# Products of constants in two waits of TensorE at the end of layer 1

## The reference

```python
x = x + L0_attn(layernorm(x)); x = x + L0_ffn(layernorm(x))
x = x + L1_attn(layernorm(x)); x = x + L1_ffn(layernorm(x))
x = x + L2_attn(layernorm(x)); x = x + L2_ffn(layernorm(x))
x = x + L3_attn(layernorm(x)); x = x + L3_ffn(layernorm(x))
```

```python
x1 = x @ sw1.T + sb1;  x2 = x @ sw2.T + sb2
sh = _ln(silu(x1) * x2, s_ln_g, s_ln_b)          # 64 wide
shared_out = sh @ sw3.T + sb3
x_moe = x[index_b, index_t]                      # 256 tokens
z = _ln(silu(h1) * h2, sel_ln_g, sel_ln_b)       # h1, h2: 8 experts x 64
expert_out = (z of the best expert) @ ew3
final_out = shared_out.at[index_b, index_t].set(shared_moe_out + expert_moe_out)
```

## Time and profile before

| | |
|---|---|
| median of 3 runs | 1480.39 us (1478.17 to 1481.1) |
| the profiled execution | 1478.13 us, with a span of 1476.3 us |
| mean granted clock of TensorE | 0.984 |
| busy share of the span | PE 95%, DVE 81%, ACT 75%, POOL 19% |
| PE idle ahead of L1485 (`turn`) | 8.0 us in 2 waits, the longest 4.5 us |

### The profile page before, as it was taken

One profiled execution on the slowest core, in us unless ns is written; L12 is line 12 of the kernel. 1 busy time (PEld: TensorE's weight loads), 2 busy tenths in 40 slices (PEclk: granted clock), 3 DMA queues, 4 the chain that ended last, 5 costly groups with the idle time before them and its releaser, 6 DMA issues.

```text
span 1476.3 us, 23605 instructions
## 1 busy us (share of the span) xinstructions
PE 1403.1 (95%) x8536; PEld 678.5 (46%) x8536; DVE 1191.5 (81%) x2559; ACT 1105.6 (75%) x2072; POOL 284.3 (19%) x239
## 2 busy tenths in 40 slices
PE   5989999999989978899999999999999998999997
PEld 4643333332248866233333333333333335565796
DVE  7699768583369978998788997888788767999997
ACT  3579888898867732787888888888888885887545
POOL 6212000000023322221111111110111012243542
PEclk9899999999999989999999999999999999999999
DMA  4166555655210001000000000000000000000000
GB/s 109 31 153 178 150 148 151 147 146 157 101 55 2 1 1 72 0 1 1 1 1 1 1 1 1 1 1 1 1 1 1 1 29 1 1 8 8 8 16 22
DMA packets 43620, 63.13 MB, mean 43 GB/s; under 512 B 5360, under 2 KB 25072, under 8 KB 43120
## 3 DMA queue, kind: packets, MB, share of 16 engines
q1 hardware_dynamic: 43504, 61.62, 15.4%
HBM read 54.27 MB, written 7.34 MB: 42 GB/s over the span
## 4 chain that ended last, share of the span: by engine, by line
PE 73%; DVE 15%; POOL 4%; ACT 3%; DMA 2%; issue 2%; SPq 1%; DVEq 0%; ACTq 0%
PE ps L2002 16%; PE ps L1992 13%; PE ps L525 8%; PE ps L515 7%; PE ps L1971 6%; PE ps L2012 4%; PE ps L1981 3%; DVE p6ac L2502 2%; PE ps L534 2%; POOL WA L2182 2%; PE ps L448 1%; POOL WA L2186 1%; DMA p1GB<-gscr 1%; DVE X L213 1%; PE ps L2395 1%
## 5 line engine op out<-in xcount | busy, mean ns | idle before, releaser
L2085 ACT ACTIVATE p4E<-ps,p4mx,p4sc 128x512 f32<-128x512 f32 x512 | 393.4, 773 | 108.8 <-DVE p4mx L2048 108.2
L2046 DVE TENSOR_REDUCE p4mx<-ps 128x2 f32<-128x1024 f32 x256 | 312.8, 1222 | 86.9 <-PE ps L1992 84.4
L2002 PE MATMUL ps<-p4E,p4vn 128*64 128x512 f32 x1024 | 249.2, 608 | 0.2 <-POOL p4vn L2107 0.2
L1992 PE MATMUL ps<-p4T 64*128 64x512 f16 x1536 | 211.0, 382 | 5.2 <-ACT p4E L2085 5.2
L2107 POOL TENSOR_TENSOR p4vn<-p4v,p4zs 128x512 f32<-128x512 f32 x64 | 66.7, 1042 | 480.0 <-DVE p4zs L2051 480.0
L752 ACT ACTIVATE p1g<-ps,WB 128x1024 f32<-128x1024 f32 x128 | 135.6, 1117 | 18.0 <-PE ps L515 18.0
L657 DVE SCALAR_TENSOR_TENSOR p1Pb<-ps,WB,p1GB 128x512 f32<-128x512 f32 x128 | 95.0, 748 | 65.1 <-PE ps L525 61.8
L515 PE MATMUL ps<-p1R,p1w1s 128*128 128x512 bf16 x512 | 131.7, 381 | 6.7 <-ACT xT L752 4.5
L1992 PEld LDWEIGHTS ps<-p4T 64*128 64x128 f16 x1536 | 54.7, 94 | 175.3 <-issue 105.1
L525 PE MATMUL ps<-p1g,WB 128*32 128x512 f32 x512 | 125.7, 599 | 1.8 <-DMA p1GB<-gscr 1.7
L525 PE MATMUL ps<-xn,WB 128*32 128x512 f32 x256 | 124.8, 599 | 0.0
(11 more groups left out here) (369 smaller groups left out, 2501.8 us busy)
## 6 DMA issues: line engine op xcount, KB each, us to landing
p1GB<-gscr SPq DMA_DIRECT2D x128, 256.0 KB
p1R<-tscr SPq DMA_DIRECT2D x64, 128.0 KB, 4.9
tscr<-p1tp SPq DMA_DIRECT2D x24, 128.0 KB, 3.1
WA<-in_w SPq DMA_DIRECT2D x1, 2632.0 KB, 18.8
WB<-in_w SPq DMA_DIRECT2D x1, 2560.0 KB, 9.3
X<-in_x SPq DMA_DIRECT2D x8, 256.0 KB, 5.7
gscr<-p1gT SPq DMA_DIRECT2D x8, 256.0 KB, 5.3
out<-X SPq DMA_DIRECT2D x7, 256.0 KB, 2.3
```

The source lines that it names most:

```text
L1992: y = p.e.matmul(ps[:, at + hh, :], t[rows, q, 128 * j:128 * j + 128], t[rows, 2 + r, :], start=o == 0, stop=o == 2)
L2002: t = p.e.matmul(ps[64 * hh:64 * hh + 64, self.bank["ctx", n], :], vn[n % 2][:, j, 64 * hh:64 * hh + 64], E[2 * (n % 3) + hh][:, j, :], st ...
L2046: v.e.tensor_reduce(m, ps[:, at:at + 2, :], AX, ALU.max).then_inc(v.own.h, v.one())
L2085: a.e.activation(self.E[2 * (n % 3) + hh][:, j, :], ps[:, at + hh, :], ACT.Exp, bias=self.mx[i][:, j, hh:hh + 1], scale=pre.sc[:, 1, 0:1], ...
```

## The change

Two of the steps `turn` get products of constants ahead of their wait: 37 ahead of `turn 6` and 28 ahead of `turn 8`, into the very bank that the step's transposes then write. Nothing else is altered.

```diff
             elif what == "turn":
                 self.released(p, (what, b))
+                if b in (6, NB):
+                    k.busy(p, bank[what, b], 37 if b == 6 else 28)
                 for j in range(self.src(b)[2]):
                     p.wait_ge(k.sem("us2"), 4 * b + j + 1)
                     t = p.e.transpose(ps[0:64, bank[what, b], cols(j)], self.us[i][:, j, :], k.ident)
```

## The result

| | before | after |
|---|---|---|
| median of 20 runs each | 1480.29 us (1476.08 to 1483.38) | 1475.14 us (1472.29 to 1481.22) |
| ratio, with its 95% interval | | 0.9971 (0.9961 to 0.9981) |
| span of the profiled execution | 1476.3 us | 1470.9 us |
| mean granted clock | 0.984 | 0.990 |

The ratio is 4.3 us (0.0029 x 1480.29), between 2.8 and 5.8. Forecast were 1477.3 us, 3.1 us less than before, and 0.50 for "faster by over 0.2%". It is faster, and the estimate lies above the forecast 3.1, though the interval holds 3.1 as well; its upper end, 0.9981, is just short of the 0.2% that was forecast. The two medians by themselves are 5.2 us apart. 1475.14 lies inside the range by 0.14 us, as its low end was 1475.0.

A forecast was written before the change was run, and what follows sets the result against it. Layer 1's end was taken as bound by DVE in the first wait and half-clock PE behind the second; weighted cases 0.7 + 1.75 + 0.7 = 3.1 us gave 1480.4 - 3.1 = 1477.3 us, range 1475.0 to 1480.4.

The forecast's parts named there:

- The batches and their waits: Ahead of `turn 6` and `turn 8`: products take 4.03 and 3.05 us, ending 0.6 and 1.0 us before the tiles come.
- No cost to the neighbours: DVE work during the two waits: added products slow it by 0, bounded at 0.1 us.
- The first part, 1.2 us: Between the two waits: DVE's waits of 0.44, 0.53 and 0.20 us for PE vanish, 1.2 us gained.
- The second part, 2.3 us: From `turn 8` to `back`: 1.3 us gained up to `made 0` and 1.0 in `made 0`, together 2.3 us.
- the first profile's own case: Both falls of the clock lie as first profiled and vanish: 3.5 us gained, weighted 0.5.
- The weights of the cases: Gains of 1.9, 3.5 and 4.5 us, by where the clock returns, weighted 0.35, 0.5 and 0.15: 3.1 us.
- the late return: Clock returns later than profiled, so `out 7` and `made 1` are slow too: 4.5 us gained, weighted 0.15.
- The short case: Low stretch of only 3.3 us behind the second wait, or early return behind the first: 1.9 us gained, weighted 0.35.
- It wins nothing: Rival: the chain does not wait for PE, or falls come at other places; time 1480.4 us, chance 0.08.
- the second fall stays: Rival: clock still falls around `turn 8`, with its ten transposes; time 1478.3 to 1479.2 us, chance 0.14.
- The overrun: Rival: first batch meets a low clock and ends up to 3.4 us late; time 1482.6 us, chance 0.06.
- Passed on: At `back` and after: nothing becomes late next, so the whole gain is handed on to the end.

The follow-up runs named there:

- e1: Kernel before plus only the 37 products ahead of `turn 6`, none ahead of `turn 8`: ratio 0.9981 (0.9962 to 0.9999).
- e2: Kernel before plus only the 28 products ahead of `turn 8`, none ahead of `turn 6`: ratio 0.9983 (0.9964 to 1.0002).
- e6: Kernel before plus 25 and 17 products ahead of the attention's fifth and seventh `score`, none at layer 1's end: ratio 0.9964 (0.9952 to 0.9976).
- e4: Changed kernel with 74 products in place of 37 ahead of `turn 6`, against the kernel before: ratio 0.9986 (0.9970 to 1.0002).
- e9: The changed kernel timed again, unaltered, against the kernel before: ratio 0.9961 (0.9949 to 0.9974).
- e12: The kernel before, unchanged, timed against itself and profiled a fourth time: ratio 1.0012 (0.9996 to 1.0029).

## Why the prediction was right, and its size too small

**The batches and their waits.** Right. 37 products take 36 paces of 0.109 us and a last one of 0.27, 4.20 us; what was left over was forecast as 0.6 and 1.0 us, and the rows have 0.33 and 0.63, counted from the end of the last product. Counted as in the forecast, from one pace behind its start, they are 0.50 and 0.81. `released` held nothing up.

**No cost to the neighbours.** Right: DVE is busy for 1191.3 us in place of 1191.5, ACT for 1106.2 in place of 1105.6, both within what the other profiles of the kernel before have (1191.3 to 1192.6 and 1105.5 to 1106.7).

**The first part, 1.2 us.** 9.39 to 8.04 us, 1.35, and `turn 6` begins 0.10 sooner. The three waits of DVE, 1.17, are gone. What comes on top fits the rows: an instruction of DVE that waits for nothing begins some 0.09 us before the end of the one ahead (539.83, where L1296 ends at 539.92), and three of them do so now. e1 and e2 show that this gain and the second's stand apart. Over the six unfilled profiles this part took 9.11 to 9.73, so 1.1 to 1.7 us.

**The second part, 2.3 us.** 7.85 to 5.54, 2.31. The forecast "some 5.5 us in place of 7.85" holds to 0.1. For the first profile's own case the sum was thus 3.5 and the section says 3.76. One reading of the forecast is off without touching the sum: the clock fell near 536.8, which is 2.2 us after the end of PE's last product at 534.6, not after its start.

**The weights of the cases.** This is the step that failed: "If instead the clock came back later than here ... 4.5 us", weighted 0.15. I had bounded the late return by the end of `made`, since work there was at full clock in the one profile that I had. In three of the six profiles with both waits unfilled the low stretch behind the second wait lasted 13.6 us and reached into `back`. There the gain is 24.43 - 19.10 = 5.3 in the section and 38.7 - 37.1 = 1.6 in `back`, 6.9 us. Over all six (22.86, 22.82, 24.43, 24.48, 21.75 and 24.42, with 1.6 added to three) the mean is 24.26 us, 5.2 more than 19.10. The two timings of the change say 4.3 (2.8 to 5.8) and 5.8 us (3.9 to 7.6), and 5.2 lies in both. So the term was mis-sized: 6.9 us for 4.5, in three of six executions for 0.15. The short case, 1.9 us at 0.35, has its like in e6 alone, 2.65 us. That the measured time stayed within the range is luck in part: its low end allowed for 4.5 us won and 0.9 for the runs, and the time lies 0.14 above it.

**The rivals.** "It wins nothing" and "the second fall stays" are out: four profiles with both batches have no fall from 500 to 556. In them ten transposes and the short wait behind the second batch did not bring the clock down: they ran at a granted clock of 1.00, the eight of `chosen` in 1.04 us against 1.91 in the earlier trace rows. So the Trainium skill's rule on transposes (TensorE: Matmul & The Clock Gate, Part 4, PE-mode transpose), that the full clock does not engage for them, did no harm here; whether transposes alone would hold the clock was not tried. The overrun did not occur at 37, and e4 shows its price at the upper clock; the rival's own case, a batch that finds the clock low, occurred in no profile at these two waits.

**Passed on.** Right. From `back` to the end it is 919.98 us before and 920.15 after in the first two profiles, and 919.81 in e9; nothing took the gain back.

## What to carry to other kernels

A wait of TensorE that another engine sets can be filled with products of constants, at no cost as long as they end before the wait does. It pays where others wait for the work behind it: the gain isn't in the wait but in what follows it at full clock. Let the products end a little before the wait does (0.3 to 0.6 us were left here), since what runs over is paid nearly in full and what is left idle too long, 2.4 us here, may let the clock fall. To size such a gain, look at more than one profile: the low stretch behind one and the same wait cost 1.4, 2.3 and 5.2 us in different executions, and with a single profile the bound must allow it to run on into the work that it shows at full clock.

## What the runs showed of the hardware

The low stretches in all of these profiles came in few lengths, near 3.4, 6.8, 10.2 (once) and 13.6 us, but for those that the end of the program cut off. The length was not set by how soon PE was busy again: in e12 PE was busy for 8.37 of the 10 us from 552 to 562 and for all of the next 3, and the clock stayed at the lower level until 565.5; in e1, with nearly the same work, it was back 3.4 us after it had fallen. Nor does the length of a wait alone settle whether the clock falls at it. In twelve of the 14 profiles PE, at the upper level, waits 1.7 us ahead of L1429 near 430 us; in seven of them the clock fell within this wait or up to 0.5 us behind it, in five it did not. At the wait of 3.05 us ahead of the fifth `score` it fell in six of the ten profiles that have this wait unfilled (within it or up to 1.5 us behind), and in the other four only behind the next wait, of 2.1 us.

In the kernel before, the runs of one program spread from 1470.46 to 1488.36 us; the falls at these two waits and behind them account for 4.3 us of such a spread (2.65 to 6.98 us over the change's section), and the start of `out 5`, from 531.25 to 537.53 us in the four profiles, for 6.3 more. The runs of the changed kernel spread as well, from 1470.98 to 1481.22 us.
